# Grouping a two-layer interaction tower by samples instead of by d, so that gathered rows are stored as they lie

## The reference

```
z  = einsum('bhd,bfd->bhfd', hidden, x).reshape(B, hidden.shape[1] * F, D)
y  = relu(einsum('bcd,oc->bod', z, w) + b[None, :, None])     # o = 128 outputs
layer 1: hidden = x (32 channels),      y -> hidden y[:, :64], direct y[:, 64:]
layer 2: hidden = 64 channels of layer 1,  y -> direct, all 128
h  = concat(direct of layer 1, direct of layer 2).sum over d   # (512, 192)
h  = concat([h, dense_ctx]); relu(h @ W_top1 + b); relu(h @ W_top2 + b); y = h @ W_top3
```

## Time and profile before

| | |
|---|---|
| median of 3 runs | 1093.7 us (1091.5 to 1093.88) |
| the profiled execution's own time | 1092.62 us |
| its span, first to last instruction | 1090.8 us |
| mean granted TensorE clock | 0.978 |
| instructions | 10701 |
| DMA over the span | 196.89 MB, 180 GB/s |

### The profile page before, as it was taken

The page is one execution under the profiler, slowest core; times in us unless marked ns, Lnnn a source line. Parts: engine busy times, 40 slices in busy tenths (PEclk is TensorE's granted clock), DMA queues, the critical chain, the costliest instruction groups (busy, mean ns, idle before and its releaser), DMA issues.

```text
span 1090.8 us, 10701 instructions
## 1 busy us (share of the span) xinstructions
PE 1025.0 (94%) x3493; PEld 651.4 (60%) x3493; DVE 944.4 (87%) x623; ACT 734.9 (67%) x907; POOL 915.5 (84%) x300
## 2 busy tenths in 40 slices
PE   2059999999999999999999999999999999999999
PEld 1025556656666666666666666666666666666664
DVE  4059999999999999999999999999998989888982
ACT  1036666767777677777777777777777777777761
POOL 7526878779999999999999899997989888988890
PEclk9569999999999999999999999999999999999999
DMA  4278777687878787778877878787777877786730
GB/s 137 55 188 200 194 186 184 180 198 190 210 178 205 183 213 187 192 191 199 207 185 192 201 181 208 182 206 194 194 184 194 204 183 187 191 208 184 183 84 1
DMA packets 142074, 196.89 MB, mean 180 GB/s; under 512 B 15858, under 2 KB 57458, under 8 KB 141891
## 3 DMA queue, kind: packets, MB, share of 16 engines
q1 hardware_dynamic: 137922, 192.01, 70.3%
q0 software_dynamic: 4096, 4.20, 1.8%
HBM read 175.18 MB, written 20.97 MB: 180 GB/s over the span
## 4 chain that ended last, share of the span: by engine, by line
PE 86%; DVE 4%; issue 4%; DMA 3%; ACT 2%; SPq 1%; DVEq 0%; ACTq 0%
PE py L610 40%; PE py L626 15%; PE py L616 14%; PE py L617 14%; DVE zf L498 2%; ACT zh L362 2%; PE py L631 1%; DMA xs<-x_dram 1%; DMA x_dram<-xf 1%; DMA xs<-in_L_rec_w 1%; PE pt L592 1%; DVE zl L515 1%; PE py L675 0%; PE pzS L675 0%; DVE zf L459 0%
## 5 line engine op out<-in xcount | busy, mean ns | idle before, releaser
L303 POOL TENSOR_TENSOR zl<-zf,zh 128x2048 fp32r<-128x2048 f32 x168 | 772.3, 4610 | 116.2 <-ACT zh L362 114.2
L498 DVE TENSOR_TENSOR zf<-xs,hid 128x2048 f32<-128x2048 f32 x256 | 583.3, 2283 | 67.1 <-ACT hid L377 51.9
L610 PE MATMUL py<-zf,wf 128*128 128x512 f32 x1072 | 485.2, 596 | 6.5 <-DVE zf L498 6.5
L362 ACT ACTIVATE zh<-zf 128x2048 fp32r<-128x2048 f32 x186 | 354.9, 1908 | 44.5 <-DVE zf L498 41.1
L610 PEld LDWEIGHTS py<-zf,wf 128*128 128x128 f32 x1072 | 203.5, 190 | 214.2 <-issue 194.2
L616 PE MATMUL py<-zh,wh 128*128 128x512 f32 x744 | 293.6, 395 | 8.7 <-ACT zh L362 8.7
L617 PE MATMUL py<-zh,wl 128*128 128x512 f32 x744 | 292.1, 393 | 0.0
L626 PE MATMUL py<-zl,wh 128*128 128x512 f32 x744 | 233.8, 436 | 0.0
L498 DVE TENSOR_TENSOR zf<-xs,px 128x2048 f32<-128x2048 f32 x64 | 146.4, 2288 | 37.8 <-DMA xs<-x_dram 35.9
L626 PEld LDWEIGHTS py<-zl,wh 128*128 128x128 f32 x744 | 135.9, 189 | 59.2 <-issue 29.2
L293 POOL DMA_INDIRECT emb<-in_tbl,idx x128 | 143.1, 1118 | 29.9 <-issue 24.5
(11 more groups left out here) (71 smaller groups left out, 439.8 us busy)
## 6 DMA issues: line engine op xcount, KB each, us to landing
xs<-x_dram SPq DMA_DIRECT2D x640, 256.0 KB
x_dram<-xf SPq DMA_DIRECT2D x64, 320.0 KB
emb<-in_tbl,idx POOLq DMA_INDIRECT x128
xs<-in_L_rec_w SPq DMA_DIRECT2D x2, 512.0 KB
xs<-in_L_rec_w SPq DMA_DIRECT2D x1, 1024.0 KB
wt<-in_W_top SPq DMA_DIRECT2D x1, 512.0 KB
wt1b<-in_W_top SPq DMA_DIRECT2D x1, 256.0 KB
wt1a<-in_W_top SPq DMA_DIRECT2D x1, 128.0 KB
```

Source lines behind the costliest of these rows:

```text
L303: pool.tensor_tensor(zl[:, q], zf[:, s], zh[:, q].bitcast(F32), ALU.subtract).then_inc(lo["P"], 1)
L362: act.activation(zh[:, q], zf[:, s], ACT.Copy).then_inc(hi, 1)
L498: dve.tensor_tensor(zf[:, slot(u)], left, right, ALU.mult).then_inc(mult, 1)
L610: mm = pe.matmul(y, wf[:, w, h], zf[:, s, h], start=first and h == 0, stop=ends and h == T - 1)
```

## The change

A group becomes NS = 8 samples by all 64 d (N = 512 still, G = 64, GC = 16). A gathered row already holds 64 d of one sample and one feature, so rows go from emb to x_dram without staging, turning or the copy xf. emb holds two chunks instead of four.

- x_dram is [NC, 160, 128 x 64]: row i of a chunk is one feature of all 128 samples, 32 KB long. A group is 2 KB out of each row. The loads are the same number, of the same size, with a pitch of 32 KB between rows.
- Gathers come in batches: 12, 12, 6 and 2 for chunk 0, then one batch per period (10 of 3 and one of 2, then 16 of 2 and 16 of 2). SP stores a batch in store_batch after a wait for its gathers, in runs of 256 bytes: a batch of 5 or more in five DMAs (one per repeat), a smaller one in one DMA per feature. That is 17 store DMAs for chunk 0, all before load_x0(0), and 2 or 3 per period later, between load_xd(g+2) and load_xe(g+1), for the batch of the period before. The first load of a chunk waits for all stores of the chunk.
- POOL waits at a batch's first gather for the batch four back, and from chunk 2 on for the stores of the chunk two back.
- add_1, add_2 and sum_d go. sum_1 and sum_2 reduce 512 elements of PSUM to 8 sums (d is contiguous) directly into zd and zsum2, per group.
- py1 gets two banks (the bank pt is gone), and P of a group waits for the group two back.

The core of the diff:

```diff
...
-ND = 4
-N = ND * P
-G = NC * D // ND
-GC = D // ND
+NS = 8
+N = NS * D
+G = B // NS
+GC = P // NS
...
+FIRST_BATCHES = [(0, 0, 12), (0, 12, 12), (0, 24, 6), (0, 30, 2)]
+PER_PERIOD = [[3] * 10 + [2], [2] * 16, [2] * 16]
+LATER_BATCHES = [(c, sum(PER_PERIOD[c - 1][:i]), n) for c in range(1, NC) for i, n in enumerate(PER_PERIOD[c - 1])]
+BATCHES = FIRST_BATCHES + LATER_BATCHES
+BATCH_SEMS = 4
+STORES = [sum(min(m, REPEATS) for b, _, m in BATCHES if b == c) for c in range(NC)]
...
-        x_dram = nc.dram_tensor("x_dram", [G, REPEATS * F, N], F32, kind="Internal")
...
+        x_dram = nc.dram_tensor("x_dram", [NC, REPEATS * F, P * D], F32, kind="Internal")
...
-            def store_x(k):
-                sp.wait_ge(xf_ready, k + 1)
-                dst = x_dram[k, 0:1, :]
-                sp.dma_start(bass.AP(tensor=dst.tensor, offset=dst.offset, ap=[[N, F], [P, ND], [F * N, REPEATS], [1, P]]),
-                             view(xf, 0, [[0, REPEATS], [1, P]])).then_inc(x_stored, 16)
+            def store_batch(n):
+                c, f, m = BATCHES[n]
+                sp.wait_ge(gathered[n % BATCH_SEMS], gathered_count(n))
+                if m < REPEATS:
+                    for i in range(m):
+                        dst = x_dram[c, f + i:f + i + 1, :]
+                        sp.dma_start(bass.AP(tensor=dst.tensor, offset=dst.offset, ap=[[D, P], [F * P * D, REPEATS], [1, D]]),
+                                     view(emb, (c % 2 * F + f + i) * D, [[0, REPEATS], [1, D]])).then_inc(x_stored[c], 16)
+                else:
+                    for i in range(REPEATS):
+                        dst = x_dram[c, i * F + f:i * F + f + 1, :]
+                        sp.dma_start(bass.AP(tensor=dst.tensor, offset=dst.offset, ap=[[D, P], [P * D, m], [1, D]]),
+                                     emb[:, c % 2, f:f + m, :]).then_inc(x_stored[c], 16)
...
+            def rows(k, r):
+                return x_dram[k // GC, r:r + 1, N * (k % GC):N * (k % GC) + N]
...
             def block_rows(k, j, t):
-                src = x_dram[k, 4 * t + j:4 * t + j + 1, :]
-                return bass.AP(tensor=src.tensor, offset=src.offset, ap=[[N, F], [4 * N, T], [1, N]])
+                src = rows(k, 4 * t + j)
+                return bass.AP(tensor=src.tensor, offset=src.offset, ap=[[P * D, F], [4 * P * D, T], [1, N]])
             def load_x0(k):
-                sp.wait_ge(x_stored, 16 * (k + 1))
+                if k % GC == 0:
+                    sp.wait_ge(x_stored[k // GC], 16 * STORES[k // GC])
                 if k >= 1:
                     sp.wait_ge(x0_ready, k)
                 sp.dma_start(x0, run_of_rows(k, 0)).then_inc(x0_in, 16)
...
+            for n in range(len(FIRST_BATCHES)):
+                store_batch(n)
             sp.wait_ge(w_turned, 6)
-            store_x(0)
             load_x0(0)
             load_xd(0)
             load_xt(0)
-            store_x(1)
+            load_xd(1)
             load_x0(1)
+            load_xt(1)
             load_xe(0)
...
             for g in range(G):
                 if g + 2 < G:
                     load_x0(g + 2)
                     load_xt(g + 2)
                     load_xd(g + 2)
-                if g + 3 < G:
-                    store_x(g + 3)
+                if g >= 1 and batch_of(g - 1) is not None:
+                    store_batch(batch_of(g - 1))
                 if g + 1 < G:
                     load_xe(g + 1)
...
+            def gather(n, i):
+                c, first, m = BATCHES[n]
+                if i >= m:
+                    return
+                f = first + i
+                if i == 0 and c >= 2:
+                    pool.wait_ge(x_stored[c - 2], 16 * STORES[c - 2])
+                if i == 0 and n >= BATCH_SEMS:
+                    pool.wait_ge(gathered[n % BATCH_SEMS], gathered_count(n - BATCH_SEMS))
                 pool.indirect_dma_start(
...
-            def stage_x(k):
-                if k >= 1:
-                    act.wait_ge(turned, k)
-                if k % GC == 0:
-                    act.wait_ge(gathered[k // GC], 16 * F)
-                cols = emb[:].rearrange("p f c d -> p f (c d)")[:, :, ND * k:ND * k + ND]
-                act.activation(stage[:], cols, ACT.Copy).then_inc(staged, 1)
-            def copy_xf(k):
-                act.wait_ge(turned, k + 1)
-                if k >= 1:
-                    act.wait_ge(x_stored, 16 * k)
-                act.activation(xf[:], pt[:, 0:P], ACT.Copy).then_inc(xf_ready, 1)
...
                 high(("C", g))
                 if g >= 1:
                     finish_2(g - 1)
-                if g + 3 < G:
-                    copy_xf(g + 3)
                 high(("B", g))
...
-            def add_1(k):
+            def sum_1(k):
                 dve.wait_ge(dir1_ready, k + 1)
-                if k >= 1:
-                    dve.wait_ge(acc1_done, k)
-                s = acc1[H:P, k // GC % 2]
...
-                    dve.tensor_tensor(s, py1[H:P], s, ALU.add).then_inc(acc1_done, 1)
-            def add_2(g):
+                dve.tensor_reduce(zd[H:P, NS * k:NS * k + NS], py1[H:P, k % 2].rearrange("p (b d) -> p b d", d=D),
+                                  AX_X, ALU.add).then_inc(sum1_done, 1)
+            def sum_2(g):
                 dve.wait_ge(dir2_ready, g + 1)
...
-            def sum_d(a, c):
-                acc, rows = ((acc1, slice(H, P)), (acc2, slice(0, P)))[a]
-                dve.wait_ge((acc1_done, acc2_done)[a], (c + 1) * GC)
-                dve.tensor_reduce((zd, zsum2)[a][rows, P * c:P * c + P], acc[rows, c % 2].rearrange("p (d b) -> p b d", d=ND),
-                                  AX_X, ALU.add).then_inc(zsum_ready, 1)
+                dve.tensor_reduce(zsum2[:, NS * g:NS * g + NS], py2[:, g % 2].rearrange("p (b d) -> p b d", d=D),
+                                  AX_X, ALU.add).then_inc(sum2_done, 1)
...
             for g in range(G):
                 products(("A", g))
-                add_1(g)
+                sum_1(g)
                 if g + 1 < G:
...
                 products(("B", g))
                 if g >= 1:
-                    add_2(g - 1)
+                    sum_2(g - 1)
                 low(("C", g))
                 products(("D", g))
-                if g % GC == 1 and g > GC:
-                    sum_d(0, g // GC - 1)
-                if g % GC == 2 and g > GC:
-                    sum_d(1, g // GC - 1)
-            sum_d(0, NC - 1)
-            add_2(LAST)
-            sum_d(1, NC - 1)
+            sum_2(LAST)
...
-            def turn_x(k):
-                pe.wait_ge(staged, k + 1)
-                if k >= 1:
-                    pe.wait_ge(xf_ready, k)
-                pe.transpose(pt[:, 0:P], stage[:].rearrange("p f d -> p (f d)"), ident[:]).then_inc(turned, 1)
...
-                if name == "P" and g >= 1:
-                    pe.wait_ge(swapped, 3 * g)
-                    pe.wait_ge(acc1_done, g)
+                if name == "P" and g >= 2:
+                    pe.wait_ge(swapped, 3 * (g - 1))
+                    pe.wait_ge(sum1_done, g - 1)
                 if name == "A" and g >= 2:
-                    pe.wait_ge(acc2_done, g - 1)
+                    pe.wait_ge(sum2_done, g - 1)
...
-            turn_x(0)
-            turn_x(1)
-            turn_x(2)
             main(("P", 0))
             tail(0)
...
-                if g + 3 < G:
-                    turn_x(g + 3)
...
-            pe.wait_ge(xf_ready, G)
             pe.wait_ge(mult, len(UNITS))
-            pe.wait_ge(zsum_ready, 2 * NC - 1)
+            pe.wait_ge(sum1_done, G)
             for m in range(4):
                 top_1_begin(m)
-            pe.wait_ge(zsum_ready, 2 * NC)
...
```

More of the change, by code:

```diff
@@ L47, in mode, with gathered_count, batch_of @@
     return "P"
[L52 to L57, removed]
+FIRST_BATCHES = [(0, 0, 12), (0, 12, 12), (0, 24, 6), (0, 30, 2)]
[4 more added lines that the diff above has]
+STORES = [sum(min(m, REPEATS) for b, _, m in BATCHES if b == c) for c in range(NC)]
+def gathered_count(n):
+    return 16 * sum(BATCHES[i][2] for i in range(n % BATCH_SEMS, n + 1, BATCH_SEMS))
+def batch_of(g):
+    return len(FIRST_BATCHES) + g if g < len(LATER_BATCHES) else None
 def period(g):
@@ L109, in sem @@
             return ctx.enter_context(nc.semaphore(name))
-        emb = sb("emb", [P, F, NC, D])
+        emb = sb("emb", [P, 2, F, D])
         idx = sb("idx", [P, NC, F], I32)
@@ L303, in low @@
                 pool.tensor_tensor(zl[:, q], zf[:, s], zh[:, q].bitcast(F32), ALU.subtract).then_inc(lo["P"], 1)
-            for f in range(F):
-                gather(0, f)
+            for n, (_, _, m) in enumerate(FIRST_BATCHES):
+                for i in range(m):
+                    gather(n, i)
             for g in range(G):
-                now = gathers(g)
+                n = batch_of(g)
                 low(("A", g))
-                for c, f in now[0:1]:
-                    gather(c, f)
+                if n is not None:
+                    gather(n, 0)
```

(16 more changed lines are left out.)

75 lines of the change are left out of this document (22 added, 53 removed).

## The result

The changed kernel takes 1102.37 us in the median of four runs (1095.39 to 1105.59), the kernel before 1093.12 us beside it (1091.5 to 1093.88): ratio 1.0076, 95% interval 1.0053 to 1.0099. It is slower by 0.8%, where 1086.7 us and faster was forecast, and it lies 3.4 us above the range. The profiled execution is the fastest of the four, 1095.39 us with a span of 1093.6, so the trace shows 2.8 us of loss against 1092.6 and not the whole 9.

What follows compares the result with a forecast made beforehand. The prediction took TensorE's nearly unbroken stream in the main loop (busy 94% of the span) as the bound. It summed -7.3 - 5.6 + 7.0 = -5.9 us on 1092.6 us to 1086.7 us, range 1078 to 1099.

Steps and rivals of the forecast that it cites:

- The loop's gains (-7.3 and -5.6): Main loop: 61 transposes gone from TensorE save 7.3 us; its stalls behind copy_xf and sum_d gone save 5.6 us.
- rival 1: VectorE: each new reduce costs 1.06 us, no longer hidden behind TensorE; total 1091.5 to 1095, say 1092.5; chance 0.13.
- The start (+7.0): Before the loop: first load waits for all chunk 0 stores; net +7.0 us, between -1.6 and +11.
- the 24 ns of a 256-byte packet: Stores to x_dram: assumed engine time per 256-byte packet, between 14.5 ns (proportional to bytes) and 29 (as for 512 bytes).
- my own slope of 0.8 us a nanosecond: Start: it grows by 0.8 us for each ns that a 256-byte store packet takes.
- Rival 2: Stores: 256-byte packets are slow, eating the gains from 31 ns; 1096 us at 36 ns, about 1154 at 60; chance 0.18.
- the third assumption: End, 18 us after the main loop (sums, top layers, output): same TensorE work before and after, taken as unchanged.
- rival 3: Loads: x_dram reads slow down with rows 32 KB apart; about 1147 us at 180 ns a packet; chance 0.05.
- a threshold of 168 ns a packet: Loop loads: 2 KB packets take at most 138 ns now; only above 168 ns is the loop DMA-bound.
- hidden: Loop stores: 1.9 or 2.9 us per period instead of 1.2, DMA share 0.84 or 0.87, so no time lost.
- the list of what would prove me wrong: First P product after 73 us, VectorE back to back with TensorE idle before it, or loop DMA share over 0.95.

Runs made afterwards that it cites:

- experiment 2: Changed kernel with rows of x_dram 34 KB apart instead of 32 KB, all else the same: 1083.24 us, ratio 0.9923 to the kernel before.
- experiment 1: The changed kernel measured again, unedited, with rows 32 KB apart: 1108.24 us, ratio 1.0141 to the kernel before.
- Experiment 5: Changed kernel (32 KB rows) with copy_x0 moved to the end of ACT's period, behind finish_dir1: 1085.0 us, ratio 0.9928 to the kernel before.
- experiment 6: Changed kernel with both 34 KB rows and copy_x0 at the end of ACT's period: 1083.22 us, ratio 0.9908 to the kernel before.
- Experiment 7: Kernel before with only x_dram's layout changed and each store sent as five DMAs: 1135.89 us at 32 KB rows, 1097.36 us at 34 KB.
- experiment 4: Changed kernel with 34 KB rows and all stores after chunk 0 left out: 1083.79 us, ratio 0.9924 to the kernel before.
- 3: Changed kernel at 32 KB rows with all stores after chunk 0 left out: 1087.46 us, ratio 0.9951 to the kernel before.

## Why the prediction was wrong

**The loop's gains (-7.3 and -5.6): right.** They can be read once the loads are mended. From the A product of the first period to that of the last it was 982.6 us before; in experiment 2 it is 969.0 us:

```profile
72.69 2.29 DVE L501 TENSOR_TENSOR zf<-xs,hid 128x2048 f32<-128x2048 f32 x1 [6.15 <-ACT hid L390]
...
1041.66 2.29 DVE L501 TENSOR_TENSOR zf<-xs,hid 128x2048 f32<-128x2048 f32 x1 [1.39 <-ACT hid L390]
```

That is -13.6 against a forecast of -12.9. Some 1.3 us of it is the wait of group 1's P product, which the forecast had counted in the start; without it -12.3. The turning is 0.13 us a period, and the stalls behind copy_xf and sum_d are gone, since TensorE has no hole at all. The reduces take 0.69 us (I took 0.70), so rival 1 falls.

**The start (+7.0): too much, it is +2.9 by the A product and +1.6 by the P product of group 1.** The term that was off is the 24 ns of a 256-byte packet. In the middle of the start's stores, 40 to 50 us of the changed kernel, the DMA view has

```profile
q1 hardware_dynamic: 8478, 2.14, 96.4%
```

that is 0.964 x 10 us x 16 engines / 8478 packets = 18 ns, near the lower bound of 14.5 and not the upper of 29. By my own slope of 0.8 us a nanosecond, 6 ns less take 4.8 us off the start, which then is +2.2. Rival 2 falls with it; in the loop of these kernels such a packet takes 19 to 20 ns. The rule of the Trainium skill (DMA: Bandwidth & Descriptors, Specifications) that an engine reads, modifies and writes below 512 bytes doesn't show in this time.

With both terms as measured the sum is 1092.6 - 13.6 + 2.9 = 1081.9, and the profiled execution of experiment 2 took 1081.99 us. As both are read from that same execution, this confirms only the third assumption, that the end is unchanged. What can be said is that the forecast, 1086.7, lies 3.5 us above the changed kernel with its loads in time (1083.24): what the sum had in it was right but for 4 to 5 us on the start, and that erred towards slow.

**The step that failed: the loads were taken as unchanged.** The sum has no term for the loads ("the same number, of the same size", says the account of the change), and their pitch was dealt with only in rival 3, at 0.05. Measured, that missing term is 25 us (experiment 1 against 2), more than all gains together. That rival named the right cause with the wrong mechanism. It asked when the DMA engines would be full and found a threshold of 168 ns a packet, under which nothing would happen. But the engines never filled (0.82 in the loop), and by the trace's events the mean 2 KB packet stayed at 131 to 138 ns in all kernels. What grew was the time from a load's issue to its last landing, by 1.2 us, with a few slow packets among many quick ones. At 32 KB the median packet takes 85 to 91 ns beside that nearly unchanged mean, at 34 KB 135; of the slowest hundredth each takes over 0.65 us in the changed kernel (up to 3.5), and over 0.53 (up to 1.6) at 34 KB. At 40 KB that bound is 0.61 us, at 64 KB 0.51, so the tail sorts these pitches as the landing does. A DMA has landed only when its last packet has, so I take the tail for the cause of the late landings; which packet held up which load was not followed. I had looked for throughput and the kernel was short of latency.

**Why 1.2 us was enough.** The prediction asked of each wait who is queued behind it, but only for waits that the change adds or takes away. copy_x0 stands ahead of high C in ACT's order in both kernels, and was never costed. Before, ACT waited there 22 times, 24.6 us in all, mostly under 2 us; that showed a load that arrives about when it is needed, with nothing to spare. Experiment 5 shows this step by itself (the late load does no harm if it is waited for elsewhere), experiment 2 shows the other (no late load, no harm), and experiment 6 that both are the same 23 to 25 us. Experiment 7 shows it without the rest of the change.

**The stores: "hidden" is right only when the loads are in time.** At 34 KB they cost nothing (experiment 4 against 2), at 32 KB 21 us (3 against 1), where x0 lands in 6.9 us with them and in 6.5 without: the last few tenths of a microsecond on a landing that is already on the edge. That also fits the spread of the changed kernel, 1095 to 1110 us over the two sets, where before stays within 4 us (1091.3 to 1095.2): with no slack small differences in landing become holes. That last is argued, not tested.

**Of the list of what would prove me wrong** nothing came true: P product at 63.2 and not after 73, VectorE not back to back, DMA share not over 0.95. The list was made from the terms I had, and the cause was in a term that I had set to zero.

**What stays open** is why 32 KB, and less so 40 KB, is slow and 64 KB is not. The runs show the slow packets and not where in memory they meet. The Trainium skill (the same page, Latency and other measured facts) reports copies slowed by a row pitch of 2 MiB (164 GB/s) and more, but not by one of 512 KiB (207 GB/s); by that rule 32 KB costs nothing. It speaks of rate, which hardly suffered here; for the landing of DMAs of 128 rows of 2 KB the measurement decides, and it says 1.2 us.

The best version of all is the changed kernel with rows 34 KB apart: 1083.24 us, 0.8% faster than before (0.6 to 0.9%).

## What to carry to other kernels

When a change alters only the addresses of a transfer, its latency is still a new number: bound it, and ask for each wait on it how much slack the trace of before shows (22 short waits are a warning) and what is queued behind. A DMA share well under 1 says nothing on that. A wait for a load belongs behind the work of its engine that doesn't need it, and padding a row by a few hundred bytes is a cheap test that takes one constant.

## What was new about the hardware

- 128 rows of 2 KB read at a pitch of 32 KB land in 6.6 to 6.9 us beside 5.4 to 5.6 us at 2 KB and 34 KB, at nearly the same mean time of a packet (131 to 138 ns). 256 bytes of padding suffice here (6.0 us); 40 KB is nearly as bad (6.6), 64 KB is not (5.8).
- A store packet of 256 bytes from SBUF takes 18 ns of an engine in the burst of the start (19 to 20 in the loop), beside 29 for 512 bytes in the first store of the kernel before.
- A reduce of 512 contiguous elements of PSUM to 8 sums takes 0.69 us, as long as an add of the same size (0.68); one that read its 512 with a hop of 128 took 1.06.
